# Sample coordinates reach all partitions by a store and two broadcast loads, not by TensorE products and a copy

## What is computed

```python
q   = gconv1x1(bn(x), qw)                       # 8 groups of 16 channels
off = tanh(pw @ gelu(depthwise 6x6 conv, stride 4, of q)) * 4     # 8 x 8 points a group, x and y
v   = grid + off;  n = 2 * v / 7 - 1            # sample points
kv  = bilinear_grid_sample(bn(x), n)            # 64 keys a group
k, val = gconv1x1(kv, kw), gconv1x1(kv, vw)
pos = grid_q - n                                # 1024 queries x 64 keys x 2
bias = mlp3(sign(pos) * log1p(abs(pos)))        # 2 -> 32 -> 32 -> 1, relu
out = softmax(q k / 4 + bias) @ val
x = x + out_w @ out + out_b
x = x + mlp(bn2(x))                             # 128 -> 512 -> 128, exact gelu
```

## Time and profile before

| | us |
|---|---|
| median of 3 runs (912.23 to 913.4) | 912.61 |
| the profiled execution: its own time | 915.55 |
| its span, from the first to the last instruction | 913.5 |
| TensorE products busy in it | 848.0 (93%) |
| VectorE busy | 711.9 (78%) |
| ScalarE busy | 657.2 (72%) |
| GpSimd busy | 71.2 (8%) |
| mean granted TensorE clock | 0.97 |

### The profile page before, as it was taken

How to read it: one execution, slowest core, us unless ns; L and a number is a source line. 1 busy time by engine, 2 the same in 40 slices (tenths; PEclk the granted TensorE clock), 3 DMA queues, 4 the chain that set the end, 5 groups by cost and what they waited for, 6 DMA issues and landing times.

```text
span 913.5 us, 33809 instructions
## 1 busy us (share of the span) xinstructions
PE 848.0 (93%) x15524; PEld 290.2 (32%) x15524; DVE 711.9 (78%) x493; ACT 657.2 (72%) x773; POOL 71.2 (8%) x40
## 2 busy tenths in 40 slices
PE   2299999899999999899999999989999999999986
PEld 1133233333333333323333333323333333333322
DVE  4699698898877688899885878889887768888811
ACT  2368678867776687887776877886777768777761
POOL 2120003210000004040000001240000000000000
PEclk8589999999999999999999999999999999999998
DMA  3301001020020101002020101002020010200000
GB/s 148 89 20 40 13 2 52 7 53 5 9 58 14 50 3 50 8 3 56 3 64 14 49 4 33 20 8 54 5 57 20 8 46 2 74 3 3 3 15 35
DMA packets 23804, 27.44 MB, mean 30 GB/s; under 512 B 15600, under 2 KB 17520, under 8 KB 23664
## 3 DMA queue, kind: packets, MB, share of 16 engines
q1 hardware_dynamic: 23664, 25.29, 10.4%
HBM read 23.05 MB, written 2.10 MB: 28 GB/s over the span
## 4 chain that ended last, share of the span: by engine, by line
issue 56%; PE 30%; POOL 6%; DVE 3%; DMA 2%; ACT 2%; SPq 0%; ACTq 0%; POOLq 0%; DVEq 0%
PE pair L797 10%; PE scores L811 9%; PE pair L792 4%; POOL conv_prod L315 3%; POOL big L422 3%; PE pair L934 2%; DVE h L589 1%; PE pair L943 1%; PE scores L821 1%; PE pair L918 1%; DMA att_den<-reciprocals_dram 1%; PE pair L900 1%; ACT h L442 1%; PE scores L906 1%; PE pair L925 0%
## 5 line engine op out<-in xcount | busy, mean ns | idle before, releaser
L442 ACT ACTIVATE h<-pair 128x1024 f32<-128x1024 f32 x512 | 496.4, 1021 | 189.9 <-PE pair L797 184.5
L589 DVE TENSOR_TENSOR h<-hx,hy 128x2048 f32<-128x2048 f32 x256 | 581.3, 2301 | 37.7 <-PE pair L797 37.4
L797 PE MATMUL pair<-h,wts 32*32 32x512 f32 x8192 | 352.3, 601 | 6.9 <-DVE h L589 6.8
L811 PE MATMUL scores<-h,wts 128*32 128x512 f32 x2048 | 277.0, 613 | 0.1
L792 PE MATMUL pair<-fy,u_rows 32*32 32x512 bf16 x4096 | 127.4, 387 | 29.6 <-DMA fy<-fy_dram 16.8
L797 PEld LDWEIGHTS pair<-h,wts 32*32 32x32 f32 x8192 | 134.0, 103 | 26.7 <-DVE h L589 10.2
L811 PEld LDWEIGHTS scores<-h,wts 128*32 128x32 f32 x2048 | 40.6, 108 | 218.5 <-issue 216.0
L792 PEld LDWEIGHTS pair<-fy,u_rows 32*32 32x32 bf16 x4096 | 40.0, 88 | 200.4 <-issue 170.0
L315 POOL TENSOR_TENSOR conv_prod<-qpad,wts 128x288 f32<-128x288 f32 x16 | 31.3, 1985 | 425.6 <-ACT qpad L469 425.6
L422 POOL TENSOR_TENSOR big<-big,hat_x 128x512 f32<-128x512 f32 x16 | 37.2, 2350 | 119.1 <-DVE big L687 119.1
L716 DVE TENSOR_REDUCE neg_max<-pair 128x8 f32<-128x512 f32 x32 | 22.1, 690 | 29.7 <-PE pair L900 29.3
(11 more groups left out here) (89 smaller groups left out, 381.1 us busy)
## 6 DMA issues: line engine op xcount, KB each, us to landing
hx<-features_dram SPq DMA_DIRECT2D x64, 128.0 KB, 2.8
hy<-features_dram SPq DMA_DIRECT2D x64, 128.0 KB, 3.2
att_den<-reciprocals_dram SPq DMA_DIRECT2D x8, 256.0 KB
wts<-weights_dram SPq DMA_DIRECT2D x2, 960.0 KB, 7.7
x<-x_dram SPq DMA_DIRECT2D x2, 512.0 KB, 5.4
fy<-fy_dram SPq DMA_DIRECT2D x64, 6.0 KB
fy<-fy_dram SPq DMA_DIRECT2D x64, 4.0 KB
fy<-fy_dram SPq DMA_DIRECT2D x64, 2.0 KB
```

What stands on the lines that cost most here:

```text
L442: emptied("z", 2 * g + j, act.activation(h2[g % H2_BUFS][:, 2 * j:2 * (j + 1)].rearrange("p r n -> p (r n)"), pair_of("z", 2 * g + j)[:], ...
L589: dve.tensor_tensor(h1[g % H1_BUFS][:].rearrange("p c (y x) -> p c y x", x=W), hx[unit % 2][:, :, t].unsqueeze(2).broadcast_to([128, CT, H ...
L797: ins = pe.matmul(z[r][32 * c:32 * (c + 1)], w(l, "w2")[key[r], key[r]], h1[g % H1_BUFS][key[r], c], start=False, stop=True)
L811: ins = pe.matmul(scores[phase % 2][32 * r:32 * (r + 1)], w(l, "w3")[:, 32 * t:32 * (t + 1)], h2[g % H2_BUFS][:, r], start=t == 0, stop=t ...
```

## The change

The coordinates now go through DRAM. SyncE stores `coord[:, 3]` (128 partitions x 8 values, each value a run of 4 bytes in DRAM, since the DRAM side is transposed) to `coords_dram`, and loads it twice as a broadcast to 128 partitions: the 512 x values into `hat_x` and the 512 y values into `key_y`. ScalarE takes |x - column| in place, in `hat_x` (`hat_x_distance`, slot 39). `spread` and `spread_out` are gone, and so is their PSUM pair. The distances move from slots 38 to 41 to slots 40 to 43, `hats` from 42 and 44 to 44 and 46, the products of the weights likewise by two slots, `sample` from 47 to 50, `sample_out` from 49 to 52, `keys_values` from 50 to 53. In the first segment the two loads stand behind the 8 feature loads and ahead of `store_fy`; in the others, between the feature store and the feature loads.

```diff
-    ("act", "offset_tanh", 0): 34, ("dve", "positions", 0): 37, ("pe", "spread", 0): 36,
-    ("act", "features", 0): 36, ("act", "spread_out", 0): 37, ("dve", "features_sign", 0): 39,
...
-    ("pe", "keys_values", 0): 50, ("act", "keys_values_out", 0): 50,
+    ("act", "offset_tanh", 0): 34, ("dve", "positions", 0): 37, ("act", "features", 0): 36,
+    ("dve", "features_sign", 0): 39, ("act", "hat_x_distance", 0): 39, ("act", "distances", 0): 40,
...
+    ("dve", "sample_out", 0): 52, ("pe", "keys_values", 0): 53, ("act", "keys_values_out", 0): 53,
...
+            def store_coords(seg):
+
+                sp.wait_ge(pos_ready, seg + 1)
+                sp.dma_start(coords_dram[seg].rearrange("n k -> k n"), coord[:, 3], allow_slow_non_contiguous=True)\
+                    .then_inc(coords_stored, 16)
+
+            def load_coords(seg):
+                if seg:
+                    for k in range(2):
+                        sp.wait_ge(bilinear_ready[k], 4 * seg)
+                sp.wait_ge(coords_stored, 16 * (seg + 1))
+                for dst, n in ((hat_x[:], 0), (key_y, PAIRS)):
+                    c = coords_dram[seg, n]
+                    sp.dma_start(dst, bass.AP(tensor=c.tensor, offset=c.offset, ap=[[0, 128], [1, 128 * PAIRS]]))\
+                        .then_inc(coords_loaded, 16)
...
                 if pair == 0:
+                    store_coords(seg)
                     store_features(seg)
+                    if seg:
+                        load_coords(seg)
                     load_features(unit)
+                    if seg == 0:
+                        load_coords(seg)
                     store_fy(seg)
...
-            def spread_out(seg):
-
-                wait_filled(act, "spread", seg)
-                here = pair_of("spread", seg)
-                emptied("spread", seg, act.activation(hat_x[:], here[:, bank(0)], ACT.Abs, bias=cst("neg_x")))
-                emptied("spread", seg, act.activation(key_y, here[:, bank(1)], ACT.Copy))
+            def hat_x_distance(seg):
+                act.wait_ge(coords_loaded, 32 * (seg + 1))
+                act.activation(hat_x[:], hat_x[:], ACT.Abs, bias=cst("neg_x")).then_inc(hat_x_distanced, 1)
 
             def distances(n):
 
-                wait_emptied(act, "spread", n // 4)
+                act.wait_ge(coords_loaded, 32 * (n // 4 + 1))
```

More of the change, by code:

```diff
@@ L79 @@
     ("dve", "conv_sum", 1): 34, ("act", "conv_gelu", 0): 33, ("pe", "offset", 0): 34,
-    ("act", "offset_tanh", 0): 34, ("dve", "positions", 0): 37, ("pe", "spread", 0): 36,
-    ("act", "features", 0): 36, ("act", "spread_out", 0): 37, ("dve", "features_sign", 0): 39,
-    ("act", "distances", 0): 38, ("act", "distances", 1): 39, ("act", "distances", 2): 40,
-    ("act", "distances", 3): 41, ("dve", "hats", 0): 42, ("dve", "hats", 1): 44,
-    ("pool", "hat_products", 0): 42, ("pool", "hat_products", 1): 44, ("dve", "hat_products", 0): 45,
-    ("dve", "hat_products", 1): 46, ("pe", "sample", 0): 47, ("dve", "sample_out", 0): 49,
-    ("pe", "keys_values", 0): 50, ("act", "keys_values_out", 0): 50,
+    ("act", "offset_tanh", 0): 34, ("dve", "positions", 0): 37, ("act", "features", 0): 36,
+    ("dve", "features_sign", 0): 39, ("act", "hat_x_distance", 0): 39, ("act", "distances", 0): 40,
+    ("act", "distances", 1): 41, ("act", "distances", 2): 42, ("act", "distances", 3): 43, ("dve", "hats", 0): 44,
+    ("dve", "hats", 1): 46, ("pool", "hat_products", 0): 44, ("pool", "hat_products", 1): 46,
+    ("dve", "hat_products", 0): 47, ("dve", "hat_products", 1): 48, ("pe", "sample", 0): 50,
+    ("dve", "sample_out", 0): 52, ("pe", "keys_values", 0): 53, ("act", "keys_values_out", 0): 53,
 }
@@ L100 @@
 PROLOGUE = {
-    "pe": ["q", "image_t", "offset", "spread", "u_rows"],
-    "act": ["q_out", "image_t_out", "conv_gelu", "offset_tanh", "features", "spread_out"] + ["distances"] * 4,
+    "pe": ["q", "image_t", "offset", "u_rows"],
+    "act": ["q_out", "image_t_out", "conv_gelu", "offset_tanh", "features", "hat_x_distance"] + ["distances"] * 4,
     "dve": ["norm1", "w1y_rows", "conv_products", "conv_products", "conv_sum", "conv_sum", "positions", "features_sign",
@@ L148 @@
 LAST_STEP = max(max(at) for at in PLAN.values())
-RELEASES = {"spread": 2, "keys_values": 5, "attend": 2, "mlp_up": 2}
-RING_STAGES = ("u_rows", "q", "image_t", "offset", "spread", "sample", "keys_values", "scores_t", "attend",
-               "project", "mlp_up", "mlp_down")
+RELEASES = {"keys_values": 5, "attend": 2, "mlp_up": 2}
+RING_STAGES = ("u_rows", "q", "image_t", "offset", "sample", "keys_values", "scores_t", "attend", "project",
+               "mlp_up", "mlp_down")
 def ring():
@@ L547, in _ @@
             stages = {"q_out": q_out, "image_t_out": image_t_out, "conv_gelu": conv_gelu,
-                      "offset_tanh": offset_tanh, "features": features, "spread_out": spread_out,
+                      "offset_tanh": offset_tanh, "features": features, "hat_x_distance": hat_x_distance,
                       "distances": distances, "attend_out": attend_out,
@@ L623, in positions @@
                 if seg >= 1:
-                    wait_filled(dve, "spread", seg - 1)
+                    dve.wait_ge(coords_stored, 16 * seg)
                     dve.wait_ge(logs_ready, 2 * seg)
@@ L862, in offset @@
                 filled("offset", seg, ins)
-            def spread(seg):
-                pe.wait_ge(pos_ready, seg + 1)
-                turn("spread", seg)
-                for n in range(2 * PAIRS):
-                    ins = pe.matmul(pair_of("spread", seg)[:, 128 * n:128 * (n + 1)],
-                                    coord[:, 3, n:n + 1].broadcast_to([128, 128]), cst("ident"), start=True, stop=True)
-                filled("spread", seg, ins)
             def sample(seg):
@@ L945, in mlp_down @@
                 filled("mlp_down", half, ins)
-            stages = {"u_rows": u_of_layer, "q": q, "image_t": image_transpose, "offset": offset, "spread": spread,
+            stages = {"u_rows": u_of_layer, "q": q, "image_t": image_transpose, "offset": offset,
                       "sample": sample, "keys_values": keys_values, "scores_t": scores_transpose, "max_off": max_off,
@@ L1055 @@
     reciprocals = nc.dram_tensor("reciprocals_dram", (2 * SEGS, G, HALF), F32, kind="Internal").ap()
-    build(nc, *args, out, features, fy_parts, reciprocals)
+    build(nc, *args, out, coords, features, fy_parts, reciprocals)
     r = run_bass_kernel_spmd(nc, [arrays], core_ids=[0])
```

7 lines of the change are left out of this document (6 added, 1 removed).

## The result

| | before | after |
|---|---|---|
| median, us | 912.74 (912.23 to 913.4, 4 runs) | 926.73 (926.35 to 928.04, 4 runs) |
| the profiled execution: own time | 915.55 | 928.04 |
| its span | 913.5 | 926.2 |
| mean granted TensorE clock | 0.970 | 0.964 |

The ratio is 1.0148, interval 1.0127 to 1.017: 14.0 us slower. The forecast of 909.2 and its range up to 915.5 are wrong, and wrong on the side of the third rival, the slow store.

The account below looks back on a forecast made before the run. TensorE, 93% busy, was taken as the bound, so time is won where it is relieved or waits less. The start's 1.4 us less 3 x 1.6 gives -3.4, from 912.61 to 909.2 us; 8-in-10 range 904 to 915.5.

Parts of the forecast that it names:

- the third rival: Coordinate store: 4-byte runs are costly, delaying the feature store and, beyond 6.9 us, ScalarE; 917.4 us at 8 us, chance 0.17.
- The store: Coordinate store in the first segment: lands in 2.3 us, before the feature store goes out, and costs nothing.
- The first segment's 1.4 us for the loads: Start: two coordinate loads ahead of the bf16 stores cost 1.8 us, 0.4 hidden; 1.4 us net, from 0.5 to 2.7.
- Step 3's wait of 0.43: First segment: TensorE's existing wait for VectorE's h1 hides 0.4 us of the loads' cost.
- The later segments' 1.6 us: Three later segment boundaries: each wins 3.2 us without a slow spell, 1.6 us with it.
- The wait ahead of step 45: Later segments: TensorE waits some 2.5 us for the PSUM pair freed by ScalarE's relu of step 44.
- the slow spell: Later segments, behind TensorE's new wait: a lower clock slows second- and third-layer products, costing 1.63 us each time.
- first rival: Later segments: the clock holds behind TensorE's new wait, so 3 x 3.2 us is won; 904.4 us, chance 0.13.
- 0.8 us ahead: Later segments: VectorE, with hats and products two slots later, is ahead by 0.8 us or more.
- the later slots: Later segments: distances two slots later meet the exp and its table load; given no cost of their own.

Follow-up runs that it names:

- kernel 1: The changed kernel with the coordinates stored as they lie, 128 runs of 32 bytes, so the output is another: 911.64 us, ratio 0.998 to the kernel before.
- kernel 2: The kernel before with only the change's coordinate store added (1,024 runs of 4 bytes, no gaps), which nobody reads: 924.36 us, ratio 1.0127.
- kernel 7: The kernel before with the unread coordinate store added, each 4-byte value in a 128-byte slot of its own in DRAM: 913.59 us, ratio 0.9999.
- kernel 3: The kernel before with only the change's later slots for distances, hats, their products, sample and keys_values: 917.04 us, ratio 1.0053.
- kernel 9: The changed kernel with coordinates turned by a TensorE product, stored as 8 runs of 512 bytes, loads moved, hats in their earlier steps: 907.71 us, ratio 0.9925 to before.
- kernel 14: The kernel before with the change's coordinate store added, unread, issued from ScalarE's queue in place of SyncE's: 925.3 us, ratio 1.0138.
- kernels 8, 12 and 16: The kernel before plus an unread store of 4-byte runs: 512 without gaps (920.22 us); 1,024 with neighbours from one partition (919.29); 1,024 in 64 of each 512 bytes (917.10).
- kernel 12: The kernel before plus an unread store of 1,024 4-byte runs without gaps, DRAM neighbours coming from one partition: 919.29 us, ratio 1.0082.
- kernel 5: The changed kernel with a packed store, one load of all 1,024 values into each partition, and ScalarE reading with a stride of 8 values: 922.75 us, ratio 1.011.

## Why the prediction was wrong

**The store (the step that failed).** The prediction took 2.3 us, "the row with the same count of runs", and 8 us as the far end. It is 10.3 to 11.2 us at the boundaries, and the feature store behind it lands 5.8 us late at the start. Neither end of the bound held what decides: both rows price runs by their number, and the price hangs on how many runs meet in 64 (perhaps 32) bytes of DRAM. The feature store's runs of 128 bytes never meet in one. The 4-byte runs of the coordinates lie side by side, 16 in each 64 bytes.

**The rival of the slow store** had the right mechanism for the start: the feature store waits, and all up to TensorE's start moves. Of TensorE's 7.7 us (25.66 against 17.93), 6.0 are the store (25.66 against 19.70 in kernel 1) and 1.8 the loads. It also foresaw that ScalarE would wait for the coordinates beyond a landing of 6.9 us: it waits 2.41, 3.40 and 2.69 us at the boundaries. It gave 917.4; missing were 2.3 to 3.2 us of the store's landing and what kernel 2 shows, a loss of 2.2, 3.5 and 2.3 us at the boundaries with nobody waiting.

**The Trainium skill's rules.** The Trainium skill ("DMA: Bandwidth & Descriptors", "Rules for kernel authors") warns of one descriptor for each element. Here the warning led the right way, but its reason doesn't carry it: kernel 7 has the same 27,964 packets as kernel 2 and costs nothing. The Trainium skill's section "Specifications" of the same page has runs under 512 bytes read, changed and written back. Runs of 4 bytes in slots of 16 to 128 bytes land in 2.5 to 2.8 us, hardly more than the feature store's 2.3, so no such price shows for a run by itself. It fits only as a price of runs that meet, in a stretch far shorter than 512 bytes.

**The first segment's 1.4 us for the loads: right in size, its parts in part by luck.** Kernel 1 shows 1.8 (19.70 - 17.93), as much as I had for the transfer alone. But half of it is the two issues: the bf16 stores are issued 6.86 us behind the feature store in place of 5.92, and the other 0.9 is their landing, 4.54 in place of 3.66. Step 3's wait of 0.43 is gone in kernel 1, but TensorE's slow stretch lasts longer there (the granted clock from 51 to 58 us is 0.83 against 0.99 in before), and the relus show nothing of those 0.4 (+1.0 at step 0, +1.35 at step 4).

**The later segments' 1.6 us: nearly right in sum, by two errors against each other.** Kernel 1, the change without its slow store, wins 1.9, 1.9 and 0.6 us at the three boundaries, 4.4 in all where I had 4.8. At the first, the relu of step 38 comes 2.29 us behind that of step 37 (forecast 2.25) and that of step 44 is 1.5 us earlier (forecast 1.2). The wait ahead of step 45 is there, 2.21 us where I had 2.5. In the timeline of TensorE in after:

```profile
196.55 0.41 PE L813 MATMUL pair<-fy,u_rows 32*32 32x512 bf16 x8 [2.21 <-ACT h L465]
196.58 1.47 PE L818 MATMUL pair<-h,wts 32*32 32x512 f32 x32
197.98 1.94 PE L832 MATMUL scores<-h,wts 128*32 128x512 f32 x8
```

Behind it the last product group runs at the low level, as in the earlier trace rows: the granted clock of after in the two stretches from there is

```profile
197.50:198.60 1.10, 1.10 (x24) 0.20 (x8) 1.10 (x2) 0.83 (x1) 1.10 (x1) 0.72 0.00 0
198.60:202.00 3.40, 3.40 (x60) 0.82 (x56) 3.40 (x2) 1.12 (x3) 3.40 (x2) 0.59 0.02 5
```

The third layer's products right behind this wait of 2.21 us take 1.94 us in place of 1.06 at three of three boundaries in after, at two of three in kernel 1 and at one of three in kernel 3. So the slow spell behind such a wait is neither sure nor excluded; forecast and first rival had taken it as always there or never. At kernel 1's first boundary there is no spell, yet 1.9 is won and not 3.2: steps 48 and 49 wait 0.45 and 0.73 us for VectorE's h1, which I had counted 0.8 us ahead. At its third the spell is longer than forecast (the second layer takes 2.56 us, the third 1.94, the next second layer 2.03), and 0.6 is left. Sum of start and boundaries in kernel 1: +1.8 - 4.4 = -2.6; its median is 1.7 below before. So with a store that costs nothing, as I had it, the forecast of -3.4 would have been close.

**What I costed at nothing and wasn't: the later slots.** I saw that the distances "now meet the exp and the load of its table" and that a wait of 2.5 us comes of it, but took it as part of a gain. Alone the slots cost 3.7 us (kernel 3), and without them the way over DRAM wins 6.3 (kernel 9). GpSimd's products at those steps take 12.0 in place of 9.45 us in kernels 1 and 3, which I had not counted; how much of the 3.7 is theirs, and how much the slow spells', is not shown.

## What to carry to other kernels

Ask of a small store not only how many runs it has, but how many of them fall into the same 64 bytes of DRAM: with 16 runs of 4 bytes there a store of 4 KB took 10 us to land, and with four or fewer about 3, at the same bytes and packets. (The stretch that counts may be 32 bytes.) Turn the data on chip first (one product and a copy of 8 rows) or leave gaps. A slow store is paid by the transfers behind it, even where nobody reads it. When an operation gets a longer path, look for an earlier start before giving all that depends on it later slots; here kernel 9 kept the slots of before, and the later slots cost 3.7 us by themselves (kernel 3).

## What the runs showed of the hardware

- Stores of 4-byte runs to DRAM without gaps land after about 10 us, 512 of them (9.9) nearly as late as 1,024 (10.3 to 11.2), and hold back a transfer issued 3.1 us behind them on the same queue (8.5 us in kernel 2 in place of 2.3) or 3.5 us behind them on another (7.6 in kernel 14). The trace books almost none of it as busy time of the DMA engines: their share is 0.00 over the last 4.7 us of that wait in kernel 2.
- The store of 1,024 runs without gaps, with neighbours from different partitions, also disturbs TensorE: the weight load of kernel 2 stops for 1.31 us "<-issue" in the middle of a product group, and at each boundary 2.2 to 3.5 us go. In kernel 14, the same store from ScalarE's queue, the boundaries lose 0.1, 3.8 and 2.6 us. The stores of kernels 8, 12 and 16 slow the start nearly as much (4.7 to 5.3 us at step 0, kernel 2 has 6.5) and cost the boundaries 0.3 us at most; that is why they are 4 to 7 us faster than kernel 2. I suspect that TensorE's instructions arrive late, since the trace has a DMA queue for instructions too (122 packets, 2.00 MB in kernel 2). The traces don't decide it: single instruction packets take up to 3.5 us in kernel 2 against 1.7 in before, but up to 3.0 in kernel 12 as well, whose boundaries lose nothing. No experiment tested this, and it stays open.
- ScalarE reads float32 with a stride of 8 values at 1.24 us for 128 x 512, against 0.72 contiguous.
- GpSimd's four products of 128 x 512 take 9.45 us in the later segments of before, 9.91 in kernel 9 and 12.04 in kernel 3; in kernel 5, with the steps of kernel 3, they take 8.99. The step alone doesn't fix it, and what does wasn't tested.
